# A new order of steps on the four engines of a two-stream adaLN kernel

## What is computed

```python
mod = silu(c) @ wmod                    # six vectors of 128 per sequence
h = layernorm(x) * (1 + ca) + sa
x = x + ga * trajectory(h, guides)      # windows of 8 differences, softmax over 64 guides
h = layernorm(x) * (1 + cb) + sb
x = x + gb * ffn(h)

def _layer(x, wqkv, qs, ksc, wo, lg, lb, w1, b1, w2, b2):   # ffn: two of these
    q, k, v = split(shift_token(x) @ wqkv)                  # 8 heads of 64
    q, k = rotary_xpos(l2norm(q) * qs, l2norm(k) * ksc)
    x = x + local_attention(q, k, v) @ wo                   # window of 64, looks one window back
    h = layernorm(shift_token(x)) * lg + lb
    a, g = split(h @ w1 + b1)
    return x + (a * gelu(g)) @ w2 + b2
```

## Time and profile before

| | us |
|---|---|
| three runs | 956.8, 960.83, 961.49 |
| median | 960.83 |
| span of the profiled execution | 957.5 |

### The profile page before, as it was taken

How to read it: one execution, slowest core, us unless ns; L and a number is a source line. 1 busy time by engine, 2 the same in 40 slices (tenths; PEclk the granted TensorE clock), 3 DMA queues, 4 the chain that set the end, 5 groups by cost and what they waited for, 6 DMA issues and landing times.

```text
span 957.5 us, 19956 instructions
## 1 busy us (share of the span) xinstructions
PE 778.8 (81%) x7439; PEld 566.8 (59%) x7439; DVE 665.8 (70%) x1575; ACT 660.0 (69%) x1545; POOL 544.8 (57%) x326
## 2 busy tenths in 40 slices
PE   5977888778788888878879779878978888878884
PEld 5855656555565755555566665556666566556652
DVE  4667775868777866676786877576677766686732
ACT  2355758777776857868775866877676877768682
POOL 3176741858675544585766643393967762675700
PEclk9888999999999999999989989999899999999997
DMA  7000000000000000000000000000000000000000
GB/s 214 1 11 13 1 2 1 2 1 2 1 1 24 2 1 12 13 1 1 1 2 1 23 1 12 12 1 1 2 1 1 12 2 12 2 1 1 1 1 22
DMA packets 12710, 10.02 MB, mean 10 GB/s; under 512 B 1088, under 2 KB 11720, under 8 KB 12616
## 3 DMA queue, kind: packets, MB, share of 16 engines
q1 hardware_dynamic: 12616, 8.77, 3.0%
HBM read 6.67 MB, written 2.10 MB: 9 GB/s over the span
## 4 chain that ended last, share of the span: by engine, by line
PE 34%; DVE 22%; ACT 18%; issue 12%; POOL 12%; DMA 0%; POOLq 0%; SPq 0%; ACTq 0%; DVEq 0%
ACT probs L1040 6%; PE pair L737 6%; POOL roots L1561 5%; PE dense L894 4%; DVE qk L1285 3%; POOL qk L1609 3%; DVE space L1486 3%; PE mixed L783 3%; PE dense L975 2%; DVE neg_max L1307 2%; DVE q_norm L1491 2%; PE dense L858 2%; PE mixed L848 2%; PE dense L859 2%; PE dense L860 2%
## 5 line engine op out<-in xcount | busy, mean ns | idle before, releaser
L1609 POOL TENSOR_TENSOR qk<-space 128x512 f32<-128x512 f32 x128 | 178.8, 1402 | 26.1 <-DVE q_norm L1491 23.0
L1561 POOL TENSOR_TENSOR roots<-powers,minus_half 128x32 f32<-128x32 f32 (+1 forms) x33 | 174.8, 5296 | 17.0 <-DVE powers L1499 16.1
L1040 ACT ACTIVATE probs<-pair,neg_max 128x128 f32<-128x128 f32 x512 | 139.1, 397 | 11.3 <-DVE neg_max L1307 10.7
L975 PE MATMUL dense<-wq_hi,h_hi 128*128 128x512 f32 x192 | 93.6, 488 | 50.1 <-DVE space L1486 24.1
L1606 POOL TENSOR_TENSOR space<-space,tables 128x512 f32<-128x512 f32 x64 | 86.9, 1358 | 58.4 <-ACT space L1167 58.4
L1486 DVE TENSOR_TENSOR space<-dense,tables 128x512 f32<-128x512 f32 x128 | 87.5, 683 | 44.0 <-ACT space L1167 43.7
L1307 DVE TENSOR_REDUCE neg_max<-pair 128x4 f32<-128x512 f32 x128 | 81.3, 682 | 31.5 <-PE pair L822 31.4
L1163 ACT ACTIVATE squares<-dense 128x512 f32<-128x512 f32 x128 | 79.0, 618 | 32.6 <-PE dense L977 32.1
L737 PE MATMUL pair<-eye_s,probs 128*128 128x128 f32 x512 | 77.8, 285 | 24.5 <-ACT probs L1040 24.4
L1491 DVE TENSOR_REDUCE q_norm<-squares 128x8 f32<-128x512 f32 x128 | 86.4, 675 | 0.0
L975 PEld LDWEIGHTS dense<-wq_hi,h_hi 128*128 128x128 f32 x192 | 38.2, 199 | 78.8 <-issue 65.6
(11 more groups left out here) (210 smaller groups left out, 1880.7 us busy)
## 6 DMA issues: line engine op xcount, KB each, us to landing
x_in<-n_L_attn_embeddings_dram SPq DMA_DIRECT2D x8, 256.0 KB, 3.0
...
```

Of the source, the lines that this page charges most:

```text
L975: pe.matmul(to[:, :], h_hi[:, rows], wq_hi[:, layer, cols], start=True, stop=False)
L1040: last = act.activation(probs[:, ring, hh, :], banks[m][:, hh * P:(hh + 1) * P], ACT.Exp, bias=neg_max[:, ring, hh:hh + 1], scale=1.0)
L1561: return pool.tensor_tensor(to, of, minus_half[0:of.shape[0], 0:of.shape[-1]], ALU.pow)
L1609: pool.tensor_tensor(qk[s][:, t, m * INNER:(m + 1) * INNER], turned_c[:, t % 2, m, :], turned_s[:, t % 2, m, :], ALU.add).then_inc(added, 1)
```

## The change

All six lists of all four engines are set anew. The same steps stand on each engine, as often as before: 685 on TensorE, 595 on ScalarE, 555 on VectorE, 243 on GpSimd. No instruction, buffer or wait is written otherwise, but TensorE's new order also deals the dense banks anew. Of TensorE's places 475 hold another step than before, of ScalarE's 410, of VectorE's 416, of GpSimd's 121. Most steps move by one or two places, none on TensorE by more than 22; VectorE's first `proj.keep` moves by 96. The SyncE queue is untouched. The new table is 30 lines longer, so everything below it has line numbers 30 higher.

```diff
@@ -48,323 +48,353 @@
 ORDER = {
...
     "dve": [
         steps("""
-        3:new.stats 3:setup.silu 3:setup.square 3:setup.guide 3:setup.mod 3:new.turn 3:setup.wide
...
+        3:new.stats 3:new.turn >2:new.stats >2:new.turn 3:setup.silu 3:setup.square 3:setup.guide
...
```

More of the change, by code:

```diff
@@ L57 @@
[L57 to L61, removed]
@@ L149 @@
         steps("""
[L150 removed]
+"""),
         steps("""
[L152 to L155 removed]
@@ L234 @@
[L234 to L237 removed]
+        <3:setup.silu <3:new.turn <3:new.dots <3:new.sims <3:setup.hi.0 <3:setup.hi.1 <3:new.mix
+        2:new.turn <3:new.stream 2:proj.split 2:proj.tile.0.0 2:proj.tile.0.1 2:proj.tile.0.2
@@ L246 @@
-        2:proj.rsqrt.0 2:new.dots 2:new.sims 2:new.weights 2:proj.keep 2:proj.unit.0 2:proj.tile.2.0
-        2:proj.tile.2.1 2:proj.tile.3.0 <3:setup.columns 2:new.gate 2:new.again 2:proj.tile.3.1 2:new.stream
-        2:proj.rsqrt.1 3:proj.keep 3:a.score.0 3:new.stats 3:proj.split 3:a.score.1 3:new.turn 3:a.unit
-        3:proj.tile.0.0 3:proj.tile.0.1 3:a.mix.0 3:proj.tile.1.0 3:proj.tile.1.1 3:proj.rsqrt.0 3:a.mix.1
-        3:proj.tile.2.0 3:proj.tile.2.1 3:new.dots 3:a.score.2 3:new.sims 3:a.score.3 3:new.weights
@@ new lines @@
+        <3:setup.lo.1 <3:setup.ff <3:setup.gate <3:new.gate <3:new.again <3:new.stream 2:proj.keep
+        2:proj.split 3:new.stats 2:proj.tile.0.0 2:proj.tile.0.1 2:proj.tile.1.0 2:proj.tile.1.1
+        2:proj.rsqrt.0 2:new.dots 2:new.sims 2:new.weights 2:proj.tile.2.0 2:proj.tile.2.1
+        2:proj.tile.3.0 2:proj.unit.0 <3:setup.columns 2:new.gate 2:new.again 3:a.score.0
+        2:new.stream 3:a.score.1 2:proj.tile.3.1 2:proj.rsqrt.1 3:proj.split 3:new.turn 3:proj.keep
+        3:proj.tile.0.0 3:proj.tile.0.1 3:proj.tile.1.0 3:proj.tile.1.1 3:proj.rsqrt.0 3:a.mix.0
@@ new lines @@
+        1:a.project 2:new.dots 2:new.sims 2:a.unit 2:new.weights 2:a.mix.0 2:proj.tile.0.0
+        2:proj.tile.0.1 2:proj.tile.1.0 2:a.mix.1 2:proj.tile.1.1 2:proj.rsqrt.0 2:proj.tile.2.0
+        2:proj.tile.2.1 2:a.score.2 2:a.score.3 2:ff.stats 2:ff.norm 2:a.mix.2 2:a.mix.3
+        2:proj.unit.0 2:proj.tile.3.0 2:proj.tile.3.1 2:proj.rsqrt.1 2:new.gate 2:new.again 2:ff.hi
+        2:new.stream 2:ff.up.0 2:ff.up.1 2:ff.up.2 3:proj.split 2:a.project 2:ff.down 3:a.score.0
+        3:a.score.1 2:store.turn 3:proj.tile.0.0 3:proj.tile.0.1 2:proj.keep 3:a.unit 3:a.mix.0
@@ new lines @@
+        2:ff.up.2 2:a.project 3:a.unit 3:proj.split 2:ff.down 3:a.score.0 3:a.score.1 2:store.turn
+        2:proj.keep 3:proj.tile.0.0 3:proj.tile.0.1 3:new.stats 3:a.mix.0 3:a.mix.1 3:proj.tile.1.0
+        3:proj.tile.1.1 3:proj.rsqrt.0 3:proj.tile.2.0 3:proj.tile.2.1 3:new.turn 3:proj.tile.3.0
+        3:a.score.2 3:ff.stats 3:a.score.3 3:a.mix.2 3:ff.norm 3:new.dots 3:a.mix.3 3:new.sims
+        3:new.weights 3:proj.unit.0 3:proj.tile.3.1"""),
+        steps("""
+        <3:a.project <3:ff.hi <3:new.gate <3:new.again <3:proj.rsqrt.1 <3:ff.up.0 <3:ff.up.1
```

573 lines of the change are left out of this document (296 added, 277 removed).

## The result

| | before | after |
|---|---|---|
| median of the runs, us | 961.16 (4 runs, 956.8 to 961.62) | 935.62 (4 runs, 934.98 to 938.37) |
| span of the profiled execution | 957.5 | 933.6 |
| TensorE's mean granted clock | 0.962 | 0.956 |

What follows compares the result with a forecast made beforehand. Trips between engines, seen as TensorE's 178.7 us of waiting, were taken to bound the kernel. Opening and first attentions -4, turn 2 -3, the rest 0: span 957.5 to 950.5, median 954 us, range 940 to 968.

Steps and rivals of the forecast that it cites:

- The rest: 0: Middle of turn 2, other turns and tail: no gain; for the tail's two saved table loads 0, bounds -2.6 and +1.3.
- What bounds the kernel: Whole run: short trips between engines set the end; any gain is part of TensorE's 178.7 us of waiting.
- Opening, -0.4: 0 to 48 us: weights 1.8 us earlier, mostly given back before `new.gate` at 36.8; -0.4 us, bounds -1.0 and 0.
- First attentions, -3.6: 48 to 145 us: second unit's turn gone -1.0, earlier weights -0.8, earlier second exponentials -1.8; bounds 0 and -7 with the opening.
- Turn 2, -3: 371 to 587 us: GpSimd and VectorE reorderings, -1 and -3.5, kept as -3 us; bounds +2.9 and -4.5.
- The two edits named: Turn 2: GpSimd's split goes behind the rotary parts of tiles 2 and 3; VectorE's maxima of tile 2 go first.
- From span to median, +3.3: Whole run: the median of the runs lies 3.3 us above the span, so span 950.5 gives 953.8.
- The gains repeat: Rival, chance 0.15: turns 1 and 3 each win turn 2's -3 and the two loads -2.6; 945 us.
- Pairs without cover: Rival, chance 0.22: paired flips leave TensorE waiting for second exponentials, 9 x 1.05 = 9.5 us; 966 us.
- signs of being wrong: Idle before flips over 30 us, turn 2 as long as before, or granted clock below 0.89 in the first 145 us.

Runs made afterwards that it cites:

- new_with_old_211_296: The new kernel with only the steps between 211 and 296 us put back in the old order; 934.92 us, ratio 0.9765 to the kernel before.

## Why the prediction was wrong

The step that failed is "The rest: 0", and with it the -3 for turn 2, which counted two edits and took all other moves for nothing. Behind 586 us the new order wins 13.2 us (interval 8 to 18) and between 528 and 586 us another 7.4; neither stands in a term. Together that is 20.6 of the 22.9 us. The terms one by one:

- **What bounds the kernel** held: trips between engines, 178.7 us of TensorE's idle time, of which 18 went.
- **Opening, -0.4.** The weights' end came earlier (the reciprocal that begins them ran at 27.77 instead of 28.59), and the gates' copy ended at 37.5, 0.7 us behind the 36.8 of the sum. But `new.gate`, which starts at 37.45 where it did before, then waits until 39.74 for the last column of `new.sum`: 2.5 us late. The term looked at VectorE and ScalarE alone. On TensorE the new order also takes the four `warm` steps away that stood ahead of the sum, which is in no term: TensorE stands 4.42 us, and the sum's products take 0.80 us instead of 0.49. The first row is of before, then two of the new kernel, then one of `new_with_old_211_296`, which has the same opening:

```profile
20.92 8.90 PE L766 MATMUL mixed<-eye_s 128*128 128x128 f32 x80
...
29.46 1.12 PE L961 MATMUL dense<-band_s,weighed 128*64 128x256 f32 x2 [4.42 <-DVE weighed L1458]
...
34.42 0.80 PE L975 MATMUL dense<-weighed,band_s 128*128 128x129 f32 x2
...
33.79 0.49 PE L970 MATMUL dense<-weighed,band_s 128*128 128x129 f32 x2
```

  In the last one the granted clock from 29.4 to 40 us was 0.84, in the new kernel 0.50, and there `new.gate` did both columns at 37.45 without a wait. So the 2.3 us are the clock under the sum. With the new opening that last column came at 39.27 to 39.86 us in six of seven traces, with the old one at 36.4 to 38.0 in all twelve; TensorE's granted clock in the first 48 us was 0.79 to 0.89 in the seven and 0.93 to 1.00 in the twelve. That the missing `warm` steps are the reason is the obvious reading; no run put them back alone.
- **First attentions, -3.6.** The gap at 65.77 was to shrink to 2.5 us and grew to 5.29, at 65.55; the same wait of the next unit, 3.10 us at 122.43, grew to 6.04 at 120.38. The second exponentials did come up (85.79 instead of 98.10). The first product with wo ended 3.2 us earlier, the next `ff.down` began 0.8 earlier (157.42 against 158.20), but with one and the same old order that `ff.down` began anywhere from 154.6 to 159.0 us in other traces, so one trace can't measure this term. The run with the new order up to 371 us has 1.0006, -1.6 to +2.8 us. The sum of both terms, -4, lies outside that.
- **Turn 2, -3.** Too small, and beyond its bound of -4.5: the two runs from 438 to 586 us have -1.8 and -7.4. The two edits named are in the first of these, whose interval takes in zero. In its trace the split came at 465.38 instead of 460.54, 4.8 us later where the bound was 2.9. The maxima ran at 489.19, 1.9 us earlier instead of 3.5, behind a `new.sims` of 5.2 us that had met GpSimd's rotary instructions. The gap of 3.43 us before the flip closed, and one of 2.49 opened before the projection at 488.82.
- **The rest, 0.** "Most steps there only move by a place or two" is true of TensorE's list (423 of 685 steps move by one place at most) and was taken for a price of nothing. Behind 586 us lie 13 us: -3.7 from 665 to 746, -2.1 from 746 to 841, -3.5 in the tail, and 3.9 that these leave, in the stretch not run or in the noise. Which waits went there is not taken apart, beyond the counts by group above (-10.5 us ahead of the output transposes, -5.0 ahead of the scores, over the whole run). Of the tail, 1.4 us are won where ScalarE's chain is shorter, and there the term had 0. (The 5.3 us that the prediction works out for two loads would, on the path, lower its sum by 5.3 us and not by 3.)
- **From span to median, +3.3.** It compared the span of one execution with the median of others; in runs that have both, the difference is 1.7 to 2.6. A small part of the miss.
- **The rivals.** "The gains repeat" had 0.15 of the chance and was right for turn 3 and the tail, not for turn 1 (-0.5 is left for all of the first 438 us); at 945 it was 9 us short because it repeated the small gain. "Pairs without cover" is half right: 27.2 - 24.5 = 2.7 us more before the flips, not 9.5. Of the signs of being wrong one came: the granted clock of the first 145 us was 0.88 (before 0.91), all of it lost in the opening, for from 48 to 145 us it was 0.93. Idle time before the flips stayed under 30. All three signs asked for losses; there was none for a gain in another place.

What I could have read in the trace of before: the 4.94 us of `new.sims` with TensorE's largest gap between 145 and 900 us behind it; the 15.4 us before the output transposes, which had a row in the groups and no term in the sum; and the 80 transposes of `warm` ahead of the sum.
